# Late weights on GpSimd's queue, the split of the maxima on GpSimd, and PSUM banks divided 3 + 2 in a two-layer cross-attention kernel

## Chip, cores and metric

The kernel runs on one core of a Trainium2 chip. The metric is the time of one execution on the device in microseconds (us), the median of several runs. Lower is better.

## What is computed

Four batches of `x` (256 x 256) and a context (512 x 256) go through two layers, all in float32:

```python
# layer 0: 16 heads of 16
q, k, v = LN1(x) @ q_w + q_b, ctx @ k_w + k_b, ctx @ v_w + v_b
attn = softmax(q k^T / 4 + mask)                    # per head, 256 x 512
h = x + (attn v) @ cproj_w + cproj_b
h = h + gelu(LN2(h) @ fc_w + fc_b) @ proj_w + proj_b      # 256 -> 1024 -> 256
# layer 1: one head of 256
p = softmax((h w_q^T)(ctx w_k^T)^T / 16)
out = h + alpha * (p (ctx w_v^T)) w_o^T
```

## The kernel before, in words

Float32 products are made of three products of split operands (high times high, high times low, low times high; `product` and `products`, lines L515 to L538). Scores of layer 0 are made of bf16 terms that small DMAs stack into `q_stack` and `k_stack` (SP, `stack_group`, L449: six DMAs of queries L436, one of the mask row L441, six of keys L447, for each group of four heads; a batch has four groups).

A group has eight slots, a batch 32, numbered from `START` = 7 to 38. In a slot PE makes the scores of tiles of the *next* group for their row maxima (`max_tile`, L570, into `s1`, two banks of PSUM), DVE takes the maximum (`take_max`, L1363), PE makes transposed scores of this group (`exp_tile`, L587, into `s2`, two banks), ACT takes their exponential (L1033), and in slots 1 and 3 PE multiplies with the values of the group before (`pv`, L598, into `om`). After the eighth maximum of a group (slot 5) DVE splits it into three bf16 parts by four small operations, each waiting for the one before (`split_max`, L1368 to L1381). In slot 6, behind its exp tile, PE transposes these (`max_rows`, L580, L584), and ACT copies them into rows of `q_stack` (L1024); the next group's exp tiles need them.

Beside it the tables at the top put other work into slots, and each engine runs its part in that order: projections of the next batch (`PRE_AT`, `V_AT`; for batch 1 `EARLY_AT`), through one bank `pre_ps`; the output path of the batch before (`POST_AT`, for batch 2 `LATE_AT`: OT normalise, NT/CP projection, ZT, F0 to F3 and PJ0 to PJ3 the MLP, CT context, HT/G/S/PT/PC/DL layer 1), through two banks `post_ps`, whose order is `POST_BANK`; in batch 0 the preparation of weights (`PREP_AT` on PE and ACT, `PREP_LOW_AT` on DVE). The last batch has its own tail (`TAIL_AT`). GpSimd (POOL) squares for the GELU (L1749), makes low parts (L1754, L1714, L1718, L1764), adds biases (L1736, L1741) and takes the power -0.5 (L1695).

The order around the start: SP issues 4 + 3 loads, then stacks groups 0 and 1 of batch 0, then four DMAs of a selection matrix (L471), loads for batch 1, group 2, six late weight loads (L476, L479), group 3, five more late loads (L481 to L485), then batch 1. ACT's `pre(1, U_Q)` (L989) waits until all stacked DMAs of batch 0 have landed, since they read the tile that it overwrites.

## Time and profile before

| | us |
|---|---|
| median of 3 runs | 321.09 |
| lowest, highest | 319.31, 323.21 |
| the profiled execution | 322.16 |
| its span, first to last instruction | 320.1 |
| mean granted clock of TensorE | 0.941 of 2.4 GHz |

Times of rows are in us from the span's start unless marked ns. "Idle before" is an engine's idle time ahead of an operation, and the arrow names what ended it. A busy PE is not a PE at its peak, since matmuls overlap.

### The profile page before, as it was taken

How to read it: one execution, taken by the hardware profiler on the slowest of the kernel's cores; microseconds unless marked ns; L12 is line 12 of the kernel's file. 1: busy time of each engine (PE TensorE's matmuls, PEld its weight loads, DVE VectorE, ACT ScalarE, POOL GpSimd, SP SyncE). 2: the span in 40 equal slices, each digit the busy share in tenths (PEclk: the TensorE clock that was granted, in tenths of full speed). 3: DMA queues.
4: the chain of work that ended last, by engine and by line, in shares of the span. 5: the costliest groups of instructions: out<-in, count | busy, mean ns of one | idle time of the engine just before them, and what ended most of it. 6: DMA issues, size and time to landing. Idle time of an engine off the chain costs nothing.

```text
span 320.1 us, 5574 instructions
## 1 busy us (share of the span) xinstructions
PE 274.5 (86%) x2073; PEld 196.7 (61%) x2073; DVE 217.0 (68%) x431; ACT 188.8 (59%) x351; POOL 87.2 (27%) x85
## 2 busy tenths in 40 slices
PE   1966875999797997998997979998999999789895
PEld 1751343576345684865775758664966786568884
DVE  5767874464867959876469678867478665364944
ACT  1643652655947587777454786966365787335722
POOL 2302000410301166670001487420030246053100
PEclk9995659695979999999999999999999999999999
DMA  5533244821153001114203011121030000000000
GB/s 172 167 122 64 82 136 137 244 70 61 61 156 127 6 28 62 64 59 131 68 33 100 15 54 59 52 82 44 34 133 0 2 0 2 2 1 0 2 33 33
DMA packets 23358, 21.60 MB, mean 67 GB/s; under 512 B 4516, under 2 KB 20468, under 8 KB 23332
## 3 DMA queue, kind: packets, MB, share of 16 engines
q1 hardware_dynamic: 20544, 17.06, 17.3%
q10 hardware_dynamic: 2788, 4.20, 3.9%
q8 instruction: 16, 0.26, 0.4%
q14 instruction: 10, 0.08, 0.1%
HBM read 10.50 MB, written 1.05 MB: 36 GB/s over the span
## 4 chain that ended last, share of the span: by engine, by line
PE 43%; DVE 18%; ACT 16%; SPq 11%; issue 5%; POOL 3%; ACTq 2%; DMA 1%; DVEq 0%
PE post_ps L532 7%; PE om L604 6%; PE pre_ps L519 6%; DVE neg_max L1365 5%; PE s L577 4%; SPq L447 4%; PE post_ps L536 4%; SPq L436 4%; PE s L594 4%; ACT probs L1033 4%; ACT q_stack L1024 2%; PE s L532 2%; DVE ft L1448 1%; PE post_ps L873 1%; POOL y_l L1754 1%
## 5 line engine op out<-in xcount | busy, mean ns | idle before, releaser
L1365 DVE TENSOR_REDUCE neg_max<-s 128x1 f32<-128x512 f32 x128 | 83.3, 683 | 16.1 <-PE s L577 15.3
L1033 ACT ACTIVATE probs<-s 128x512 f32<-128x512 f32 x128 | 75.6, 599 | 28.7 <-PE s L594 28.0
L577 PE MATMUL s<-k_stack,q_stack 97*128 97x512 bf16 x128 | 51.6, 431 | 12.0 <-DVE neg_max L1365 6.3
L594 PE MATMUL s<-q_stack,k_stack 109*128 109x256 bf16 x256 | 52.7, 291 | 6.2 <-ACT probs L1033 5.0
L594 PEld LDWEIGHTS s<-q_stack,k_stack 109*128 109x128 bf16 x256 | 21.5, 104 | 22.3 <-ACT probs L1033 7.5
L577 PEld LDWEIGHTS s<-k_stack,q_stack 97*128 97x128 bf16 x128 | 12.7, 102 | 36.5 <-DVE neg_max L1365 20.2
L604 PE MATMUL om<-probs,vals 128*17 128x256 f32 x512 | 34.9, 393 | 0.0
L1695 POOL TENSOR_TENSOR ln<-ln,minus_half 128x2 f32<-128x2 f32 x8 | 5.6, 702 | 66.2 <-DVE ln L1313 66.0
L604 PEld LDWEIGHTS om<-probs,vals 128*17 128x17 f32 x512 | 12.1, 98 | 13.9 <-issue 7.9
L1391 DVE TENSOR_TENSOR y_l<-post_ps,y_h 128x512 fp32r<-128x512 f32 x12 | 8.3, 690 | 16.9 <-ACT y_h L1047 16.9
L1024 ACT ACTIVATE q_stack<-om 13x1024 bf16<-13x1024 bf16 x16 | 16.3, 1016 | 5.1 <-PE om L584 4.7
L1047 ACT ACTIVATE y_h<-post_ps 128x512 fp32r<-128x512 f32 x12 | 7.0, 595 | 17.5 <-PE post_ps L536 14.2
L1448 DVE SCALAR_TENSOR_TENSOR ft<-ft,fx 128x512 f32<-128x512 f32 x9 | 12.0, 1331 | 6.8 <-POOL ft L1749 6.8
L1714 POOL TENSOR_TENSOR kf<-kf,kp 128x512 f32<-128x512 f32 x7 | 8.1, 1161 | 28.7 <-ACT kp L1016 28.7
L1754 POOL TENSOR_TENSOR y_l<-fx,y_h 128x512 fp32r<-128x512 f32 x9 | 11.6, 1286 | 14.5 <-ACT y_h L1086 14.5
L1749 POOL TENSOR_TENSOR ft<-fx 128x512 f32<-128x512 f32 x9 | 9.4, 1040 | 15.6 <-ACT fx L1060 15.6
L532 PE MATMUL post_ps<-aT_h,wf_h 128*128 128x256 f32 x48 | 13.6, 316 | 0.0
L532 PE MATMUL post_ps<-wp_h,y_h 128*128 128x256 f32 x48 | 13.5, 314 | 0.0
L1736 POOL TENSOR_TENSOR h<-h,cb 128x512 f32<-128x512 f32 x3 | 3.8, 1281 | 34.0 <-DMA h<-in_x_dram 34.0
L532 PE MATMUL post_ps<-aT_h,wf_l 128*128 128x256 f32 x48 | 11.8, 280 | 0.0
L532 PE MATMUL post_ps<-wp_l,y_h 128*128 128x256 f32 x48 | 11.8, 279 | 0.0
L1344 DVE SCALAR_TENSOR_TENSOR kf<-pre_ps,bk,mask_f 128x512 f32<-128x512 f32 x7 | 5.2, 747 | 7.8 <-PE pre_ps L519 7.7
(329 smaller groups left out, 705.1 us busy)
## 6 DMA issues: line engine op xcount, KB each, us to landing
k_stack<-kp SPq DMA_DIRECT2D x96, 64.0 KB
q_stack<-qp SPq DMA_DIRECT2D x90, 32.0 KB
cx<-in_ctx_dram SPq DMA_DIRECT2D x4, 512.0 KB, 4.5
pcx<-in_ctx_dram ACTq DMA_DIRECT2D x3, 512.0 KB, 3.7
xz<-in_x_dram SPq DMA_DIRECT2D x5, 256.0 KB, 2.9
raw_late<-in_L_xattn_fc_w_dram SPq DMA_DIRECT2D x1, 1024.0 KB, 5.1
raw_late<-in_L_xattn_proj_w_dram SPq DMA_DIRECT2D x1, 1024.0 KB, 9.6
h<-in_x_dram ACTq DMA_DIRECT2D x3, 256.0 KB, 2.7
```

The lines of the kernel that those rows point to most:

```text
L436: sp.dma_start(q_stack[i * HD:(i + 1) * HD, group(g), :], qp[rows_of(g), part, g // 2, :]).then_inc(stacked[g], 16)
L447: sp.dma_start(k_stack[i * HD:(i + 1) * HD, group(g), :], kp[rows_of(g), part, c, :]).then_inc(stacked[g], 16)
L519: mm = pe.matmul(o, wi(w[a], k), vi(v[c], k), start=start and k == 0 and i == 0, stop=stop and k == n - 1 and i == 2)
L532: pe.matmul(o, wi(w[a], k), vi(v[c], k), start=start and i == k == a == c == 0, stop=False)
L577: pe.matmul(s1[:, s % 2, :], q_stack[0:ROW_MAX, hd, chunk(t)], k_stack[0:ROW_MAX, hd, :], start=True, stop=True).then_inc(s1_full, 1)
L594: mm = pe.matmul(s2[:, s % 2, i * LQ:(i + 1) * LQ], k_stack[:, hd, chunk(k)], q_stack[:, hd, :], start=True, stop=True)
L604: mm = pe.matmul(om[32 * j:32 * j + VW, 0:LQ], vals[:, k, j * NG + g, :], probs[:, g % 2, j, k, :], start=k == 0, stop=k == TK - 1)
L1024: act.activation(q_stack[ROW_MASK:ROWS, g * GH:(g + 1) * GH, :], om_rows[ROW_MASK:ROWS, :].unsqueeze(1).to_broadcast([ROWS - ROW_MASK, GH, ...
L1033: act.activation(probs[:, g % 2, s // 2, k:k + 2, :], s2[:, s % 2, :].rearrange("p (k n) -> p k n", k=2), ACT.Exp).then_inc(s2_free, 1)
L1365: dve.tensor_reduce(neg_max[:, g % 2, s % 2, s // 2:s // 2 + 1], s1[:, s % 2, :], AX.X, ALU.max, negate=True).then_inc(s1_free, 1)
L1448: dve.scalar_tensor_tensor(f, f, 1.0 / GELU_CUBIC, fx[i % 3], ALU.add, ALU.mult).then_inc(cube, 1)
L1754: pool.tensor_tensor(lo, fx[i % 3], hi.bitcast(F32), ALU.subtract).then_inc(y_split, 1)
```

## The change

1. SP's selection matrix goes out as one DMA with a broadcast instead of four.
2. The eleven late weight loads leave SP's queue. GpSimd issues six behind its first `split_max`, four in slot 8 and one in slot 14.
3. `split_max` moves from DVE to GpSimd, first thing in its slot, with the same four operations.
4. `s1` has three banks (batch 3 and the first eight tiles use two of them), and a max tile waits for the tile that had its bank. `pre_ps` and `post_ps` become two banks `work_ps` that alternate in the order of PE's program; while PJ holds one, all others use the other. Each use waits until the use before it on its bank has been emptied.
5. Slots move by one to three in all tables. ctx transposes come ahead of the vector transposes at the start.

```diff
-PRE_AT = {7: U_CT, 8: U_CT + 1, 9: U_ZT, 11: U_Q, 14: U_K, 22: U_K + 1}
-V_AT = {36: 0, 38: 1}
+PRE_AT = {7: 0, 8: 1, 9: 2, 10: 3, 14: 4, 19: 5}
+V_AT = {37: 0, 38: 1}
-POST_AT = {7: "OT", 8: "NT", 9: "CP", 11: "ZT", 13: "F0", 15: "F1", 16: "F2", 19: "F3", 20: "PJ0",
-           21: "PJ1", 22: "CT0", 23: "PJ2", 24: "CT1", 25: "PJ3", 26: "CX", 27: "HT", 28: "G", 30: "S0",
-           31: "S1", 33: "PT0", 34: "PT1", 36: "PC", 37: "DL"}
+POST_AT = {7: "OT", 8: "NT", 9: "CP", 12: "ZT", 14: "F0", 15: "F1", 17: "F2", 19: "F3", 20: "PJ0", 21: "PJ1",
+           22: "CT0", 23: "PJ2", 24: "CT1", 25: "PJ3", 26: "CX", 27: "HT", 29: "G", 30: "S0", 31: "S1",
+           34: "PT0", 35: "PT1", 36: "PC", 37: "DL"}
-EARLY_AT = {7: 0, 8: 1, 9: 2, 11: 3, 14: 4, 22: 5}
+EARLY_AT = {8: 0, 9: 1, 10: 2, 12: 3, 15: 4, 22: 5}
-PREP_AT = {16: "WT", 18: "WO", 19: "WC", 21: "CB", 22: "WF0", 24: "WF1", 28: "WP0", 30: "WP1", 38: "END"}
-PREP_LOW_AT = {17: "WT", 19: "WO", 21: "WC", 22: "CB", 24: "WF0", 26: "WF1", 31: "WP0", 36: "WP1"}
+PREP_AT = {16: "WT", 18: "WO", 20: "WC", 21: "CB", 22: "WF0", 24: "WF1", 25: "WP0", 28: "WP1", 40: "END"}
+PREP_LOW_AT = {17: "WT", 19: "WO", 21: "WC", 23: "CB", 24: "WF0", 27: "WF1", 32: "WP0", 35: "WP1"}
...
-        s1 = ps("s1", [P, 2, 512])
+        s1 = ps("s1", [P, 3, 512])
-        pre_ps = ps("pre_ps", [P, 512])
-        post_ps = ps("post_ps", [P, 2, 512])
+        work_ps = ps("work_ps", [P, 2, 512])
+        spare_ps = s1[:, 2, :]
...
+                    for use in new:
+                        bank = 1 - held if held is not None else 1 - bank
+                        uses.append(use + (bank,))
+                        if use[0] == "post" and use[2] == W_PJ:
+                            held = bank
+                    if step == "PJ3":
+                        held = None
...
+        def await_bank(eng, kind, b, n):
+            bank = work_bank(kind, b, n)
+            on = [u for u in WORK if u[3] == bank]
...
+        def s1_bank(b, s):
+            return s % 2 if b == B - 1 or NS * b + s < SLOTS else (NS * b + s) % 3
...
-                for g in range(NG):
-                    sp.dma_start(k_stack[ROW_MAX:ROWS, group(g), :], sel[:]).then_inc(sel_in, 16)
+                sp.dma_start(k_stack[ROW_MAX:ROWS, :, :].rearrange("p (g h) n -> p g (h n)", g=NG),
+                             sel[:].rearrange("p h n -> p (h n)").unsqueeze(1).to_broadcast([3 * GH, NG, GH * LK])).then_inc(sel_in, 16)
...
-                for i, w in ((2, l1_v), (3, l1_o)):
-                    sp.dma_start(raw_l1[i], w.rearrange("(c p) n -> p c n", p=P)).then_inc(wo_in, 16)
-                for g in range(NG):
-
-                    sp.dma_start(raw_c[rows_of(g), g // 2, :], cproj_w.rearrange("(j x d) n -> x j d n", j=GH, x=NG)[g]).then_inc(wc_in, 16)
                 stack_group(0, 3)
-                sp.dma_start(raw_f, fc_w.rearrange("(c p) n -> p c n", p=P)).then_inc(wf_in, 16)
...
-                await_(pe, s1_free, n - 1)
+                await_(pe, s1_free, s1_before(b, SLOTS * g + s))
...
-                    if s == SPLIT_AT:
-                        split_max(nb, ng)
...
+            def attend(b, g, s):
+                nb, ng = ahead(b, g)
+                if s == SPLIT_AT and nb < B:
+                    split_max(nb, ng)
...
                 key_low(0, 1)
+                pool.wait_ge(dve_const, 2)
+                split_max(0, 0)
+                for i, w in ((2, l1_v), (3, l1_o)):
+                    pool.dma_start(raw_l1[i], w.rearrange("(c p) n -> p c n", p=P)).then_inc(wo_in, 16)
+                for g in range(NG):
+
+                    pool.dma_start(raw_c[rows_of(g), g // 2, :], cproj_w.rearrange("(j x d) n -> x j d n", j=GH, x=NG)[g]).then_inc(wc_in, 16)
+                for s in range(START):
+                    attend(0, 0, s)
...
+            def load_late(at):
+                if at == LOAD_AT:
+                    pool.dma_start(raw_f, fc_w.rearrange("(c p) n -> p c n", p=P)).then_inc(wf_in, 16)
+                    pool.dma_start(cb[:], cproj_b.rearrange("(o n) -> o n", o=1).partition_broadcast(P)).then_inc(bc_in, 16)
+                    pool.dma_start(pb[:], proj_b.rearrange("(o n) -> o n", o=1).partition_broadcast(P)).then_inc(bc_in, 16)
+                    pool.dma_start(alpha_c[:], alpha.partition_broadcast(P)).then_inc(bc_in, 16)
+                elif at == LOAD_AT + 6:
+                    pool.dma_start(raw_p, proj_w.rearrange("(c p) n -> p c n", p=P)).then_inc(wp_in, 16)
```

## Rows read from the trace of the kernel before

**Rows 1.** The page: busy time by engine, and the granted clock.

```profile
PE 274.5 (86%) x2073; PEld 196.7 (61%) x2073; DVE 217.0 (68%) x431; ACT 188.8 (59%) x351; POOL 87.2 (27%) x85
...
PEclk9995659695979999999999999999999999999999
```

**Rows 2.** Windows by stage: PE, PEld, DVE, ACT, POOL busy, clock, DMA share, GB/s.

```profile
55.00:93.00 38.00, 33.53 (x214) 19.97 (x214) 21.72 (x39) 25.19 (x44) 7.63 (x7) 0.78 0.41 129
93.00:160.00 67.00, 60.99 (x507) 44.05 (x506) 50.13 (x96) 45.10 (x86) 24.14 (x20) 1.00 0.22 69
```

**Rows 3.** Timeline of SP's queue: start, duration, instruction, count.

```profile
26.87 3.15 SPq L471 DMA_DIRECT2D k_stack<-fx  x4
...
40.54 0.59 SPq L476 DMA_DIRECT2D raw_late<-in_L_xattn_w_v_dram  x1
41.17 0.47 SPq L476 DMA_DIRECT2D raw_late<-in_L_xattn_w_o_dram  x1
41.68 2.42 SPq L479 DMA_DIRECT2D raw_late<-in_L_xattn_cproj_w_dram  x4
...
48.70 3.74 SPq L447 DMA_DIRECT2D k_stack<-kp  x6
```

**Rows 4.** The chain that ended last, at its first piece on L471.

```profile
26.87 0.83 SPq L471
```

**Rows 5.** Timelines of PE and ACT, 38 to 60 us.

```profile
38.52 0.39 PE L594 MATMUL s<-q_stack,k_stack 109*128 109x256 bf16 x2 [0.25 <-ACT probs L1033]
39.66 0.32 PE L584 MATMUL om<-ident_b,max_cols 128*109 128x128 bf16 x2 [0.76 <-DVE max_cols L1381]
...
42.31 1.04 PE L577 MATMUL s<-k_stack,q_stack 97*128 97x512 bf16 x2 [1.67 <-DMA k_stack<-kp]
...
56.51 0.61 PE L594 MATMUL s<-q_stack,k_stack 109*128 109x256 bf16 x2 [3.81 <-ACT probs L1033]
...
54.40 0.84 ACT L994 ACTIVATE qf<-pre_ps,bq 128x256 f32<-128x256 f32 x2 [4.69 <-DMA k_stack<-kp]
```

**Rows 6.** Windows of 2 us after the two stalls.

```profile
42.00:44.00 2.00, 1.69 (x7) 1.11 (x8) 1.95 (x4) 0.14 (x1) 0.00 (x0) 0.50 0.81 261
...
58.00:60.00 2.00, 2.00 (x7) 1.22 (x7) 0.29 (x1) 0.27 (x1) 1.16 (x1) 0.50 0.58 131
```

**Rows 7.** Groups of the page by line: the first and last operation of DVE's split.

```profile
L1375 DVE CAST max_cols<-neg_max 128x8 bf16<-128x8 f32 x16 | 3.6, 226 | 0.6
...
L1381 DVE TENSOR_TENSOR max_cols<-max_rest,max_cols 128x8 bf16<-128x8 f32 x16 | 2.8, 178 | 0.6
```

**Rows 8.** Tile `max_cols`: who waited for the split, us and times.

```profile
  PEld om L584: 8.5, 9
  PE om L584: 5.7, 9
```

**Rows 9.** POOL's timeline: small operations, the power, and two widths of tensor_tensor.

```profile
1.25 0.29 POOL L1770 TENSOR_SCALAR_AFFINE_SELECT ident<-ident 128x128 f32<-128x128 f32 x1 [0.24 <-POOL sel_small L1768]
1.50 0.18 POOL L1773 TENSOR_SCALAR_AFFINE_SELECT sel_small<-sel_small 12x4 f32<-12x4 f32 x1
...
40.83 0.72 POOL L1695 TENSOR_TENSOR ln<-ln,minus_half 128x2 f32<-128x2 f32 x1 [13.15 <-DVE ln L1313]
...
131.65 1.76 POOL L1741 TENSOR_TENSOR h<-h,pb 128x512 f32<-128x512 f32 x1
136.46 1.27 POOL L1754 TENSOR_TENSOR y_l<-fx,y_h 128x512 fp32r<-128x512 f32 x1 [3.05 <-ACT y_h L1086]
...
141.45 2.38 POOL L1764 TENSOR_TENSOR pc_l<-pcx,pc_h 128x1024 fp32r<-128x1024 f32 x1 [0.68 <-ACT pc_h L1098]
```

**Rows 10.** What PE waited for from 93 to 160 us.

```profile
PE s L577 <- DVE neg_max L1365: 2.7, 6, 1.1
PE pre_ps L553 <- DVE cT_l L1335: 0.7, 1, 0.7
...
PE om L584 <- DVE max_cols L1381: 0.6, 2, 0.3
```

More of the change, by code:

```diff
@@ L315, in pre_use, with work_uses @@
             return PRE_USES * b + pre_place(b, n) + 1
+        def work_uses():
+            uses, bank, held = [], 1, None
+            for n in FIRST_ORDER:
+                if pre_place(0, n) % 3:
+                    uses.append(("pre", 0, n, pre_place(0, n) % 3 - 1))
+            for b in range(B):
+                for at in range(START, LAST_SLOT if b == B - 1 else START + NS):
+                    new = []
+                    if b < B - 1 and at in pre_at(b + 1):
+                        new.append(("pre", b + 1, pre_at(b + 1)[at]))
+                    if b < B - 1 and at in V_AT:
+                        new.append(("pre", b + 1, U_V + V_AT[at]))
+                    step = steps_at(b - 1).get(at) if b > 0 else None
+                    new += [("post", b - 1, n) for n in STEP_USES.get(step, ())]
+                    if b == 0 and PREP_AT.get(at) in PREP_USES:
+                        new.append(("prep", 0, PREP_AT[at]))
+                    for use in new:
[5 more added lines that the diff above has]
+                        held = None
+            return uses
@@ new lines, in s1_bank, with s1_before, s2_bank, s2_before @@
+        def s1_bank(b, s):
+            return s % 2 if b == B - 1 or NS * b + s < SLOTS else (NS * b + s) % 3
+        def s1_before(b, s):
+            n = NS * b + s
+            return max([i for i in range(max(0, n - 3), n) if s1_bank(i // NS, i % NS) == s1_bank(b, s)], default=-1) + 1
+        def s2_bank(b, s):
+            return s % 2
+        def s2_before(b, s):
+            n = NS * b + s
+            return max([i for i in range(max(0, n - 3), n) if s2_bank(i // NS, i % NS) == s2_bank(b, s)], default=-1) + 1
@@ L1695, in rstd, with split_max @@
                 pool.tensor_tensor(st[:, :, 8], st[:, :, 8], minus_half[:], ALU.pow).then_inc(done, 1)
+            def split_max(b, g):
+                step = 3 * (NG * b + g)
+                part = [max_cols[:, :, ROW_MAX + i:ROWS:3] for i in range(3)]
+                neg = neg_max[:, g % 2, :, :]
+                pool.wait_ge(s1_free, NS * b + SLOTS * (g + 1))
+                await_(pool, rows_ps, NG * b + g)
+                pool.tensor_copy(part[0], neg).then_inc(max_step, 1)
+                pool.wait_ge(max_step, step + 1)
+                pool.tensor_tensor(max_rest[:], neg, part[0], ALU.subtract).then_inc(max_step, 1)
+                pool.wait_ge(max_step, step + 2)
+                pool.tensor_copy(part[1], max_rest[:]).then_inc(max_step, 1)
+                pool.wait_ge(max_step, step + 3)
+                pool.tensor_tensor(part[2], max_rest[:], part[1], ALU.subtract).then_inc(max_split, 1)
+            def attend(b, g, s):
+                nb, ng = ahead(b, g)
+                if s == SPLIT_AT and nb < B:
+                    split_max(nb, ng)
             def mask_row_of(b):
@@ L1810, in tail_slot @@
                     tail(step)
-            def iteration(b, first, last):
-                for at in range(START, START + NS):
+            def load_late(at):
[6 more added lines that the diff above has]
+                    pool.dma_start(raw_p, proj_w.rearrange("(c p) n -> p c n", p=P)).then_inc(wp_in, 16)
+            def iteration(b, first, last):
+                for at, ab, g, s, attends in slots(b, last):
+                    if attends:
+                        attend(ab, g, s)
+                    if first:
+                        load_late(at)
                     if not last and at == LN1_AT:
```

140 lines of the change are left out of this document (72 added, 68 removed).

## The prediction

> **What bounds the kernel now.** Read the page first: PE is busy 86% of the span, the others at most 68%, and the granted clock falls to about half in several slices of the first 93 us, then stays at full [rows 1]. Then the windows by stage. A full batch (93 to 160 us) takes 67.0 us with PE busy 61.0, so there PE sets the pace and some 6 us of it are waits. Batch 0's stage from 55 to 93 has PE busy 33.5 of 38 at a mean clock of 0.78 [rows 2]. So the middle has little air, and the start has much. SP's queue then shows the start: it issues DMAs back to back, here from 26.87 to 52.4 us, and between the stacks of groups 1, 2 and 3 lie the selection matrix (four, 3.15 us) and six late weights (0.59 + 0.47 + 2.42, with gaps 3.60 us) [rows 3]. Two waits come of that: PE stands 1.67 us at 42.31 for keys of group 2, and ACT stands 4.69 us until 54.40 for group 3's keys before it may overwrite the query tile; PE stands 3.81 us behind ACT's exponentials [rows 5]. After each, PE runs at 0.50, the lower of its two levels (1.2 GHz) [rows 6].
>
> **The change part by part** (terms against the profiled execution, 322.16 us, 1.07 above the median; span 320.1, the rest lies around it).
>
> *SP's queue.* Six issues go: 3.60 us. Three of four selection issues go: 3.15 less one of 0.83 [rows 4], 2.3 us, if one DMA of four times the rows issues like one of them; if it issued like all four, nothing. So group 2's last keys come 2.3 us earlier than 42.3 and group 3's land 5.9 us before 54.3, at 48.4. The queries of batch 1 move from slot 11 to 12, which at the pace of the rows is about 49 us, so ACT then waits for nothing or under 1 us. PE gets back 1.67 + 3.81 = 5.5 us. Bounds: 3 (selection saves nothing, and what comes next is the PE product in front of ACT's wait) and 5.5. What is late next is the pace of PE, DVE and ACT inside the slots. The five later loads moved off SP stand behind group 3, ahead of batch 1's stacks, which wait for their parts anyway: 0.
>
> *Clock.* The exp tile at 56.51 and six key matmuls behind it run at half speed until about 61.4: 4.9 us of PE work, 2.4 if PE never went idle. After the first stall PE also runs low, from 42 to 48, but short gaps (0.76 and 0.25 us at 38.5 to 39.7 [rows 5]) stay, so I take 0.6 of up to 2.8. Together -3.0, bounds 0 and -5.2.
>
> *The split on GpSimd.* No row shows these operations there. Before, four of about 0.2 us [rows 7] and their hand-overs, 0.85 us from the last maximum to PE's transpose. GpSimd's tensor_tensor takes 1.27 us at 512 and 2.38 at 1024 elements [rows 9]: 2.2 ns an element and 0.16 fixed, so 0.18 at 8 elements, as its 12x4 operation takes 0.18. Its hand-over is up to 0.24. A split is then 4 x 0.18 + 3 x 0.24 + 0.1 = 1.5 us, 0.65 more. Bounds: 0 more (hand-overs as short as DVE's), and like the power's 0.72 each [rows 9], 3.7 us, 2.85 more; below nothing by 0.3 a group where DVE was late itself (0.6 us for two groups [rows 10]). I take 0.65, nearest the rows of like size. PE waited for the split in 9 of 16 groups [rows 8]; the other seven had cover (a projection or output product in slot 6). Two of the nine lie before 42 us: +1.3, now on the path. One is in the rest of batch 0, two in each of the two full batches, two in the last: each +0.65. Queued behind the waiting split on GpSimd are squares, low parts and biases; in slot 21 the order is bias (1.76 us), key rest, split, low part of F2, and DVE and PE's PJ2 wait for that last one. DVE gives up 0.85 x 16 = 13.6 us of a 217 us engine, which alone moves nothing.
>
> *GpSimd's DMAs.* The first six follow the first split, about 32.3, and the second split is due at 39.66 less 0.85 = 38.8 [rows 5]: 6.5 us for six issues. On SP these took 0.47 to 0.6 [rows 3], 3.6 in all, and hide. Above 1.1 us each they delay the second split. No row shows an issue on GpSimd; bounds 0.4 and 2.4 us (its longest operation [rows 9]), the first costing 0, the second 14.3 - 6.5 = 7.8 us. I take under 1.1, cost 0. The four of slot 8 have until the query rest, two slots later at least. The Trainium skill ("DMA: Bandwidth & Descriptors", sections Specifications and SWDGE vs HWDGE vs iDMA) says that a DMA from GpSimd has its descriptors written by software there, about 1 us to the first byte against 0.6; and ("SBUF — State Buffer", Who interferes with whom) that certain copies on VectorE lock it out meanwhile. If those 0.4 us more stood on GpSimd for each issue, six would take 6.0 and the sum stays; the second rule speaks against the change, and no row of before can show it, since GpSimd issues nothing there.
>
> *Banks.* PE waits 2.7 us of a full batch for a maximum to free one of two score banks [rows 10]; with three, I take all of it as gone. Against it, shared work banks: in slot 7 the second OT transpose now waits for the context part to be drained, where PE waited 0.7 us for DVE's cT_l one step later [rows 10]; F1 waits for the keys' drain, PJ0 for the second keys'. I take +0.7 for the first, 0 for the others, which have a whole product as cover. Per full batch: -2.7 + 0.7 + 2 x 0.65 = -0.7, two of them -1.4; bounds -3.3 and +3 each (two missed drains of 1.5 us). The last batch keeps two score banks: 2 x 0.65 less 0.6 for a freer DVE, +0.7, bounds -1 and +2.
>
> *Rest of batch 0.* DVE's splits go and the weight steps are spread, and PE's score banks are three, with one split +0.65: I take -1.0 net, bounds 0 and -3. The remaining slot moves by one are taken at 0.
>
> Sum: -5.5 + 1.3 - 3.0 - 1.4 + 0.7 - 1.0 = **-8.9 us**. 322.2 - 8.9 = 313.3 for an execution like the profiled one, 1.1 less against the median: **312.2 us**. About 1% (3.2 us) is what a measurement of this kernel can tell from no change.
>
> **The rivals.**
> (a) *Only the stalls go.* The lower clock stays where it was, because PE still has short gaps, and splits and banks cancel: -5.5 + 1.3 and nothing else, 317. For it: the clock fell to about half four separate times in the first 93 us, some without a long stall [rows 1]. Against: PE was really idle for 3.8 us before the second [rows 5].
> (b) *GpSimd's queue is late with DMAs.* At 2 us an issue the second split is 5.5 us late, and PE with it, which eats the stall: 312.2 + 5.5 = 317.7, and the four of slot 8 could cost as much again, 321. For it: no row of its issues. Against: SP's rows.
> (c) *Shared work banks bite.* +3 us instead of -0.7 in both full batches: 312.2 + 7.4 = 319.6. For it: DVE drains late where it is full.
> (d) *Slower: GpSimd's split costs like its power.* 2.85 more instead of 0.65 for each of the nine exposed groups is +19.8, and I let the seven covered ones pay half of 2.85, +10.0: 312.2 + 29.8 = 342. It decides from 0.65 + 8.9 / 9 = 1.6 us more than DVE, 0.63 us an operation. For it: the two-element power at 0.72. Against: 0.18 for a 12x4 operation, and two widths of tensor_tensor that extrapolate to it [rows 9]. The Trainium skill ("GPSIMD Engine Reference", Performance versus the Vector engine) puts an elementwise operation at about twice VectorE's time; a split of 1.7 us would add 0.2 to each of nine groups and give 314.0. No row of before shows GpSimd at 8 elements in a tensor_tensor.
>
> **How the numbers follow.** The forecast, with its own range of 305 to 316.5, 0.58; (a) 0.14; (b) 0.10; (c) 0.08; (d) 0.10, since it decides at a price between two rows. Faster by over 1% (under 317.9): 0.58 + 0.12 of (a) + 0.05 of (b) + 0.01 of (c) = 0.76. Within 1%: 0.02 + 0.04 + 0.06 + 0.01 of (d) = 0.13. Slower: the rest, 0.11. The range is 303 (stalls, clock and banks all at their good ends would be under 300, together unlikely) to 320, which leaves (d) and a little of (b) and (c) outside.
>
> **What would show it.** SP's queue free by about 47 to 49 us; no wait of ACT over 1 us at the query step of batch 1, none of PE for keys of group 2; exp of slot 13 near 52; clock not at 0.5 from 56 to 61. GpSimd's four split operations about 0.2 us each, and the time from the last maximum to PE's transpose about 1.5 us. In a full batch, DVE's maxima no longer end a wait of PE, and the batch takes 66 to 66.5 us. It is wrong if GpSimd's issues fill the time to its second split, if full batches take over 68 us, or if ACT waits at another place for what SP now sends earlier.

## The result, and the profile after

The changed kernel takes **317.93 us** (median of 20 runs, 314.11 to 321.68) against 319.76 us of the kernel before (20 runs beside it, 318.43 to 323.21); the ratio is 0.9885, 95% interval 0.9851 to 0.9919, so some 3.7 us (1.2%) less. A ratio leaves out the runs of the slower of this kernel's two states (8 of these 20), so it can differ from the ratio of two medians, and where they differ it is the ratio that a reading rests on. The forecast was 312.2 us, 8.9 us less. The time lies in its range, but the gain is less than half of what was put down.

The profiled execution after takes 315.73 us with a span of 313.5, against 322.16 and 320.1. So the pair of traces shows 6.6 us, more than the medians (1.8) or the ratio (3.7) do: the one after is among the shortest of its runs, the one before is 2.4 us over its median of 20. Sizes are therefore read below from several profiles, never from this pair alone.

The page of the kernel after, its parts 1 and 2:

```profile
PE 272.2 (87%) x2073; PEld 198.5 (63%) x2073; DVE 207.1 (66%) x367; ACT 188.3 (60%) x351; POOL 110.3 (35%) x160
...
PEclk9999579987889999999999999999999999999999
```

DVE lost 9.9 us and POOL gained 23.1 (15.5 the split's 64 operations, 7.6 the eleven DMA issues): that work moved as planned [rows 1]. PE is still the pace. Six slices lie below full clock, as before, but they are less deep: up to the transpose of slot 38 the mean clock is 0.87 (0 to 95.5 us) against 0.81 (0 to 98.4 us). The windows of the two full batches, to be set beside [rows 2]:

```profile
95.50:160.60 65.10, 59.40 (x498) 44.73 (x497) 45.67 (x78) 43.97 (x85) 27.66 (x35) 1.00 0.20 63
160.60:226.90 66.30, 59.96 (x499) 44.75 (x498) 46.16 (x79) 44.06 (x85) 28.32 (x36) 1.00 0.17 57
```

SP's queue after, with one issue for the selection rows (0.88 us, against 3.15 for four in [rows 3]) and group 3's keys at 44.66, where they had begun at 48.70:

```profile
27.86 0.88 SPq L538 DMA_DIRECT2D k_stack<-fx  x1
...
44.66 3.75 SPq L515 DMA_DIRECT2D k_stack<-kp  x6
```

ACT and PE there, to be set beside [rows 5]: ACT's wait at the query step is 2.24 us for 4.69, PE's wait for keys of group 2 is 0.48 for 1.67, and its wait for ACT 1.91 for 3.81.

```profile
52.53 0.84 ACT L1058 ACTIVATE qf<-work_ps,bq 128x256 f32<-128x256 f32 x2 [2.24 <-DMA k_stack<-kp]
```

```profile
42.75 0.60 PE L640 MATMUL s<-k_stack,q_stack 97*128 97x512 bf16 x2 [0.48 <-DMA k_stack<-kp]
...
54.65 0.39 PE L657 MATMUL s<-q_stack,k_stack 109*128 109x256 bf16 x2 [1.91 <-ACT probs L1097]
```

GpSimd's timeline: the second split, and ahead of it the six DMA issues that stand behind the first split.

```profile
33.26 0.95 POOL L1861 DMA_DIRECT2D raw_late<-in_L_xattn_w_v_dram  x1
34.21 0.73 POOL L1861 DMA_DIRECT2D raw_late<-in_L_xattn_w_o_dram  x1
34.94 2.52 POOL L1864 DMA_DIRECT2D raw_late<-in_L_xattn_cproj_w_dram  x4
40.62 0.20 POOL L1750 CAST max_cols<-neg_max 128x8 bf16<-128x8 f32 x1 [3.17 <-DVE neg_max L1429]
40.91 0.20 POOL L1752 TENSOR_TENSOR max_rest<-neg_max,max_cols 128x8 f32<-128x8 f32 x1
41.18 0.20 POOL L1754 CAST max_cols<-max_rest 128x8 bf16<-128x8 f32 x1
41.46 0.21 POOL L1756 TENSOR_TENSOR max_cols<-max_rest,max_cols 128x8 bf16<-128x8 f32 x1
```

An operation is 0.20 us and the next starts 0.28 later: 1.1 us for an undisturbed split, where 1.5 was forecast. The six issues end at 37.5, 3.2 us before the split is due.

What PE waited for over the whole span (engine, line, releaser, total us, times, longest):

```profile
PE om L647 <- POOL max_cols L1756: 10.2, 7, 2.1
...
PE s L640 <- DVE neg_max L1429: 4.2, 14, 0.6
PE work_ps L702 <- DVE cT_l L1399: 3.5, 2, 1.8
```

The first line is the surprise: fewer waits for the split than before (7 for 9) and nearly twice the time (10.2 for 5.7 us, [rows 8]). If a split is only 0.25 us longer than on DVE (1.1 for 0.85), something else is late. The third line has no counterpart before. The timelines of POOL, DVE and PE at 82 us, and of PE at 99, show both:

```profile
82.34 1.13 POOL L1750 CAST max_cols<-neg_max 128x8 bf16<-128x8 f32 x1 [3.35 <-DVE neg_max L1429]
```

```profile
82.19 1.21 DVE L1543 SCALAR_TENSOR_TENSOR wp_l<-raw_late,wp_h 128x1024 fp32r<-128x1024 f32 x1
```

```profile
84.37 0.32 PE L647 MATMUL om<-ident_b,max_cols 128*109 128x128 bf16 x2 [2.12 <-POOL max_cols L1756]
...
99.03 0.66 PE L702 MATMUL work_ps<-ident,oT 128*128 128x128 f32 x4 [1.77 <-DVE cT_l L1399]
```

GpSimd's cast of 8 elements lasts 1.13 us and ends (83.47) just after DVE's subtraction (83.40), which had started 0.15 earlier. The kernel before has the same thing the other way round: DVE's cast of 8 elements takes 0.57 us twice (132.88 and 199.8) where the other fourteen take 0.18, and the first ends (133.45) just after the bias on GpSimd, which runs from 131.65 to 133.41 [rows 9].

```profile
132.88 0.57 DVE L1375 CAST max_cols<-neg_max 128x8 bf16<-128x8 f32 x1
```

That is why the mean of this cast stands at 226 ns in [rows 7], beside 178 for the last operation of the split. And in the changed kernel's slot 7 the second transpose of the output path takes the bank that a projection product has just filled, and waits 1.77 us until DVE has drained it.

### The profile page after: what moved, and what is told of

Read it like the earlier page. It is cut to its first block, busy times and chain, and to the rows that moved or that the text cites. A ratio compares the mean times of both kernels' runs of the same rounds, so it can differ in the third digit from the quotient of the medians.

```text
span 313.5 us, 5588 instructions
## 1 busy us (share of the span) xinstructions
PE 272.2 (87%) x2073; PEld 198.5 (63%) x2073; DVE 207.1 (66%) x367; ACT 188.3 (60%) x351; POOL 110.3 (35%) x160
## 3 DMA queue, kind: packets, MB, share of 16 engines
q0 software_dynamic: 1152, 3.15, 3.3%
HBM read 10.50 MB, written 1.05 MB: 37 GB/s over the span
## 4 chain that ended last, share of the span: by engine, by line
PE 52%; POOL 10%; ACT 10%; SPq 10%; DVE 7%; issue 6%; DMA 2%; ACTq 2%; POOLq 0%; DVEq 0%
PE work_ps L590 10%; PE om L667 7%; PE work_ps L577 6%; PE s L640 5%; PE work_ps L594 5%; PE s L657 5%; SPq L515 5%; SPq L504 3%; DVE neg_max L1429 3%; ACT probs L1097 2%; POOL y_l L1820 2%; PE s L590 2%; POOL kf L1780 1%; ACT q_stack L1088 1%; DMA k_stack<-kp 1%
## 5 line engine op out<-in xcount | busy, mean ns | idle before, releaser
L640 PE MATMUL s<-k_stack,q_stack 97*128 97x512 bf16 x128 | 49.3, 418 | 6.6 <-DVE neg_max L1429 4.2
L657 PEld LDWEIGHTS s<-q_stack,k_stack 109*128 109x128 bf16 x256 | 20.9, 103 | 21.1 <-ACT probs L1097 6.6
L1750 POOL CAST max_cols<-neg_max 128x8 bf16<-128x8 f32 x16 | 5.5, 344 | 66.4 <-DVE neg_max L1429 66.4
L1111 ACT ACTIVATE y_h<-work_ps 128x512 fp32r<-128x512 f32 x12 | 7.2, 597 | 16.2 <-PE work_ps L594 14.5
L1440 DVE TENSOR_TENSOR y_l<-work_ps,y_h 128x512 fp32r<-128x512 f32 x12 | 8.3, 688 | 12.0 <-ACT y_h L1111 12.0
L1497 DVE SCALAR_TENSOR_TENSOR ft<-ft,fx 128x512 f32<-128x512 f32 x9 | 10.0, 1110 | 6.5 <-POOL ft L1815 6.5
L647 PE MATMUL om<-ident_b,max_cols 128*109 128x128 bf16 x32 | 5.0, 241 | 10.2 <-POOL max_cols L1756 10.2
L590 PE MATMUL work_ps<-wp_h,y_h 128*128 128x256 f32 x48 | 13.3, 310 | 0.5 <-DVE kf L1408 0.5
L590 PE MATMUL work_ps<-aT_h,wf_h 128*128 128x256 f32 x48 | 12.8, 300 | 0.0
L1408 DVE SCALAR_TENSOR_TENSOR kf<-work_ps,bk,mask_f 128x512 f32<-128x512 f32 x7 | 5.2, 746 | 10.6 <-PE work_ps L577 10.3
L590 PE MATMUL work_ps<-wp_l,y_h 128*128 128x256 f32 x48 | 11.8, 279 | 0.0
```

What stands on the lines that cost most here:

```text
L590: pe.matmul(o, wi(w[a], k), vi(v[c], k), start=start and i == k == a == c == 0, stop=False)
L640: pe.matmul(s1[:, s1_bank(b, SLOTS * g + s), :], q_stack[0:ROW_MAX, hd, chunk(t)], k_stack[0:ROW_MAX, hd, :], start=True, stop=True).then_ ...
L657: mm = pe.matmul(s2[:, s2_bank(b, SLOTS * g + s), i * LQ:(i + 1) * LQ], k_stack[:, hd, chunk(k)], q_stack[:, hd, :], start=True, stop=True)
```

## The experiments

All times below are medians. Each group of kernels was measured beside runs of the kernel before, which the third column gives; only kernels with the same one can be compared directly. What tells most are the places of the maxima's transposes in each profile, for they cut the span into stages: the one of slot 22 and of slot 38 of batch 0, the same slot of the next batches, the last one, and the end. (The one of slot 14 is left out, since the new slots move a projection step across it.)

| kernel | us | before | slot 22 | to slot 38 | full batches | last rows | to the end |
|---|---|---|---|---|---|---|---|
| before | | | 77.2 | 21.2 | 66.9, 66.9 | 28.2 | 59.7 |
| after | 317.93 | 319.76 | 72.7 | 22.8 | 65.1, 66.3 | 29.1 | 57.5 |
| e_ctrl | 318.03 | 321.5 | 71.1 | 23.4 | 66.5, 66.3 | 29.1 | 57.5 |
| e_vec_first | 318.37 | 321.5 | 71.6 | 24.6 | 66.0, 67.6 | 29.1 | 57.5 |
| e_fc_sp | 318.59 | 321.5 | 71.6 | 24.8 | 66.2, 67.7 | 29.1 | 57.4 |
| e_split_dve | 319.44 | 321.5 | 71.5 | 20.6 | 67.7, 68.8 | 28.2 | 58.3 |
| e_banks_back | 318.81 | 321.16 | 73.3 | 24.6 | 65.9, 65.9 | 29.1 | 57.5 |
| f_sp_only | 314.19 | 321.16 | 70.0 | 19.6 | 67.0, 66.9 | 28.2 | 59.7 |
| e_pre_late | 315.71 | 321.16 | 71.8 | 23.4 | 64.3, 66.6 | 29.1 | 57.5 |
| e_wp33 | 315.79 | 321.16 | 72.2 | 22.9 | 66.6, 66.3 | 29.1 | 57.5 |
| h_pool | 319.30 | 320.99 | 69.9 | 22.0 | 68.0, 68.0 | 29.1 | 59.4 |
| h_hyb | 319.50 | 320.99 | 70.0 | 23.1 | 68.0, 68.1 | 29.1 | 59.4 |
| h_new | 315.17 | 320.99 | 73.5 | 20.9 | 64.4, 66.6 | 29.1 | 57.5 |
| f_sp_again | 315.90 | 320.99 | 70.0 | 21.0 | 67.0, 66.9 | 28.2 | 59.8 |
| g_best | 310.75 | 320.14 | 72.2 | 21.8 | 64.4, 66.4 | 29.1 | 57.6 |
| g_dve_old | 320.70 | 320.14 | 71.9 | 23.1 | 68.2, 68.0 | 28.2 | 57.8 |
| g_tail | 313.56 | 320.14 | 72.0 | 22.2 | 66.9, 67.0 | 28.1 | 57.7 |
| g_late33 | 314.00 | 320.14 | 71.6 | 23.7 | 64.4, 66.5 | 29.1 | 57.5 |

The two columns of batch 0 scatter by 1 to 2 us each between profiles of one kernel (f_sp_only and f_sp_again, after and e_ctrl), with the clock. Together they scatter more: g_tail has the batch 0 of f_sp_only, and its slot 38 stands at 94.2 where those two have 89.6 and 91.0. The last two columns agree within 0.1.

**The changed kernel once more (e_ctrl).**

> The changed kernel once more, unchanged. Its profiled execution had a clock of 0.962 and a span 6.6 us under the one profiled before, while the medians differ by 1.8 us and the ratio is 0.9885. Theory (the runs scatter with the granted clock): a ratio of 0.985 to 0.992, and a second profile whose span is 2 to 5 us longer, at a clock of 0.93 to 0.95, with the difference before 100 us. Rival (the profiled pair is typical): ratio 0.98 and the same span within 1 us.

318.03 us, ratio 0.9892 (0.9843 to 0.9941). The same time again, so the missing 5 us is no chance of the first runs. Its ratio and clock (0.950) are the theory's, but its span is not: 313.9 us, 0.4 longer than the first profile's, as the rival had it. New in its profile is a stretch at half clock right behind the wait of slot 7, which the first profile didn't have. Its 2 us windows, PE's busy time first and the clock in the third column from the end:

```profile
96.00:98.00 2.00, 0.23 (x3) 0.05 (x1) 0.79 (x2) 1.15 (x2) 0.00 (x0) 1.00 0.00 0
98.00:100.00 2.00, 2.00 (x8) 1.38 (x9) 1.31 (x5) 0.57 (x1) 0.00 (x0) 0.53 0.03 8
100.00:102.00 2.00, 2.00 (x12) 1.88 (x11) 1.38 (x3) 0.78 (x3) 0.00 (x0) 0.62 0.59 223
```

PE stands almost still from 96 to 98, then works at 0.53. That makes the full batch 1.4 us longer than in the first profile (66.5 for 65.1).

**Three guesses: the start's order, four loads, the split.**

```diff
 # e_vec_first: the vector rows' transpose goes ahead of pre(0, U_CT), as before the change
 # e_fc_sp: SP issues these again, behind group 3's stack
-                if at == LOAD_AT:
-                    pool.dma_start(raw_f, ...)   # and cb, pb, alpha_c
+                sp.dma_start(raw_f, ...)         # and cb, pb, alpha_c
 # e_split_dve: the whole of split_max runs on VectorE again
-                if s == SPLIT_AT and nb < B:
-                    split_max(nb, ng)            # GpSimd
+                    if s == SPLIT_AT:
+                        split_max(nb, ng)        # VectorE, after its maxima
```

> The changed kernel, with the vector transposes ahead of the context transposes again. Theory: the early start of PE at 4.9 us is what leaves the key product at 11.1 us at the lower clock (0.43 us from matmul to matmul where it was 0.23), so the keys' first DMA goes out 0.9 us later; undone, the first six-fold key stack starts at 14.6 instead of 15.6 and the kernel gains about 1 us. Rival: the clock there is chance, and nothing moves.

> The changed kernel, with fc_w, cb, pb and alpha back on SP's queue behind group 3's stack (the six first late loads and proj_w stay on GpSimd). Theory: the 1 MB of fc_w issued at 42.5 us travels ahead of group 3's stack and makes its last DMA land 4.5 us after its issue instead of 2.4; back behind it, ACT's wait at the query step of batch 1 falls from 2.2 us to under 0.5 and the kernel gains 1.5 to 2 us. Rival: the landing is slow because of the small stacking DMAs themselves; nothing moves.

> The changed kernel, with the split of the maxima back on DVE (same slots, banks and queues; GpSimd waits for the first split before its six loads). Theory: on GpSimd a split costs PE 0.3 to 1.1 us more at each of the 7 groups where it waits, and 2.1 us once where a two-input DVE operation blocks it, so the kernel gains 3 to 4 us. Rival: DVE needs its 0.85 us a group itself, and the kernel loses 2 us or more.

318.37, 318.59 and 319.44 us: ratios 0.9874, 0.988 and 0.9864, each interval over the others. The first two theories fall: slot 22 comes at 71.6 with both, 71.1 without. The first key stack of six starts at 15.01 us in e_vec_first and in e_ctrl alike, and ACT's wait at the query step is 1.82 us in e_fc_sp for 1.80 in e_ctrl, both ended by PE. The third is the telling miss. With the split on DVE the end of batch 0 comes 2.4 to 3.4 us earlier (92.1 for 94.5 and 95.5), as expected, but the full batches take 67.7 and 68.8 us (65.1 to 66.5 in the two profiles of the changed kernel). The gain is given back there, and the 3 to 4 us that were expected don't come.

**What each part does alone (e_banks_back, f_sp_only, e_pre_late, e_wp33).**

```diff
 # e_banks_back
-        s1 = ps("s1", [P, 3, 512])
-        work_ps = ps("work_ps", [P, 2, 512])
+        s1 = ps("s1", [P, 2, 512])
+        work_ps = ps("work_ps", [P, 3, 512])     # bank 2 for projections, POST_BANK for the rest
 # f_sp_only, from the kernel before
-                for g in range(NG):
-                    sp.dma_start(k_stack[ROW_MAX:ROWS, group(g), :], sel[:]).then_inc(sel_in, 16)
-                sp.dma_start(raw_l1[i], ...)     # and the four of raw_c
+                sp.dma_start(k_stack[ROW_MAX:ROWS, :, :]..., sel[:]...to_broadcast(...)).then_inc(sel_in, 16)
+                pool.wait_ge(max_split, 1)       # GpSimd, at the end of its prologue
+                pool.dma_start(raw_l1[i], ...)   # and the four of raw_c
 # e_pre_late
-PRE_AT = {7: 0, 8: 1, 9: 2, 10: 3, 14: 4, 19: 5}
+PRE_AT = {8: 0, 9: 1, 10: 2, 11: 3, 14: 4, 19: 5}
 # e_wp33, in PREP_LOW_AT
-32: "WP0"
+33: "WP0"
```

> The changed kernel with the banks of the kernel before: two banks for the maxima's scores, one bank of their own for the projections, two for the output path. The slots' new order, the late weights on GpSimd's queue and the split on GpSimd stay. Theory (the shared banks cost about what the third bank brings): the wait of 1.77 us of the transpose of slot 7 for VectorE's cT_l goes back to some 0.7, no stretch at half clock follows at 98 to 106, the waits for neg_max of 2.7 us a batch come back, a full batch takes 66 to 67 us (65.1 and 66.3 in the changed kernel) and the time is 317 to 320 us. Rival one (the third bank is a gain of 1.4 us and more): 319.5 to 321. Rival two (the shared banks are the loss that ate the forecast): 314 to 316.5, and less scatter between runs.

> The kernel before with the changes on SyncE's queue alone: one DMA for the selection rows, and the six late weight loads issued by GpSimd after the first split; the split on VectorE, the banks and the slots as before. Theory (this part carries nearly all of the gain, and the rest of the change sums to about nothing): the wait of 4.69 us of ScalarE at the query step falls to about 2, the transpose of group 2's maxima comes at 54 to 55 us where before it came at 59.9, the full batches keep 66.9 us, and the time is 315.5 to 317.5 us, 3.5 to 5.5 under the kernel before. Rival (the banks and GpSimd's split bring the gain of the full batches, and this part alone 1 to 2 us because the clock gives the rest back): 318.5 to 320.

> The changed kernel with the four first projection steps of the batches ahead one slot later (slots 8 to 11 in place of 7 to 10), so that the second transpose of the output path in slot 7 no longer takes the bank that a projection product has just filled. Theory (the shared bank's wait of 1.77 us at 99 and 164 us is a real loss and sets off the half clock that follows in some executions): the wait falls under 0.7 us, no slice at half clock at 98 to 106, a full batch takes 64 to 65 us, and the time is 314.5 to 316.5 us with less scatter. Rival (the wait only moves to the next bank user in slot 8 or 9, or the late projections are missed by the group after them): 317.5 to 320.

> The changed kernel with VectorE's subtraction for the low part of the projection weights one slot later (slot 33 in place of 32), so that it doesn't run beside GpSimd's first cast of the split at 82 us. Theory (the two engines block each other there): that cast takes 0.2 us in place of 1.13, TensorE's wait for the split at 84.4 falls from 2.12 to about 1.2 us, and the rows of the maxima that stand at 84.4 move by about 0.9; in the time about 0.9 us, which is near what the rounds can tell. Rival (the cast is late for another reason, its wait for the last max or the queue of GpSimd): it still ends at the same time and the wait stays 2.1.

*f_sp_only*: 314.19 us, 7.0 under the kernel before by the medians and 3.5 by the ratio (0.9891, 0.9829 to 0.9952); measured again it has 315.90, 5.1 under by the medians and 5.2 by the ratio (0.9838, 0.9787 to 0.989). Its slot 38 is 8.8 and 7.4 us earlier than before (4.2 in g_tail), and nothing else moves: full batches of 67.0 and 66.9. ACT's wait at the query step is down to 1.05 us, and what ends it is no longer a DMA:

```profile
51.13 0.84 ACT L989 ACTIVATE qf<-pre_ps,bq 128x256 f32<-128x256 f32 x2 [1.05 <-PE pre_ps L514]
```

PE's wait for ACT there, 3.81 us before and 1.91 and 1.47 in the two profiles of the changed kernel, is 0.16. So SP's part alone gives about as much as the whole change or more. Which of the two, these runs leave open: its medians are 2 to 4 us lower and its spans (311.4, 312.9) 0.6 to 2.5 us shorter than those of the changed kernel (313.5, 313.9), but the two never ran side by side, and the intervals of their ratios overlap (0.9891 and 0.9838 against 0.9885 and 0.9892). It leaves out of the change the split, the banks, the slots and the five later loads' move.

*e_banks_back*: 318.81 us, ratio 0.9988 (0.9933 to 1.0043). The theory's numbers hold: slot 7's wait is 0.7 us, PE's waits for `neg_max` come back (2.0 us in a full batch, where the changed kernel has 1.0 and the kernel before 2.7), and the full batches take 65.9 and 65.9 against 65.1 to 66.5. In the full batches third score bank and shared work banks cancel, nearly. Its ratio is 1% above the changed kernel's all the same, and in its profile that lies in batch 0 (slot 38 at 97.9); whether the banks help there stays open.

*e_pre_late*: 315.71 us (0.9925, 0.988 to 0.997), so in the range by its time, while the ratio shows no gain over the changed kernel's 0.9885. The waits of its first full batch:

```profile
PE s L640 <- DVE neg_max L1429: 1.5, 2, 1.2
PE om L647 <- POOL max_cols L1756: 1.4, 1, 1.4
PE work_ps L577 <- DVE zT_l L1399: 1.1, 1, 1.1
```

L702 is gone from the list; 1.1 us of it is back at the query product, which now starts one slot nearer its operand. The batch takes 64.3 us, the shortest of all until then. The second takes 66.6, no less than the changed kernel's 66.3, for there the waits that come back (1.1 for `zT_l`, 0.6 more for `neg_max`, 0.7 for `z`) eat the gain. And the clock: six profiles have the wait of slot 7, each of them twice. Behind seven of these twelve waits PE runs at half clock within 1.5 us, behind four of the first and three of the second. Of the twelve profiles without this wait (the kernel before among them) none shows half clock at this place. Only g_dve_old shows any in the full batches, both times right at the end of a wait of 2.5 us for the split in slot 22, and e_split_dve has the same once. That such a wait brings the clock down in some executions is as near shown as profiles can.

*e_wp33*: 315.79 us (0.9934, 0.9888 to 0.998), again no gain by the ratio. POOL's cast and PE's transpose:

```profile
82.23 0.20 POOL L1750 CAST max_cols<-neg_max 128x8 bf16<-128x8 f32 x1 [3.70 <-DVE neg_max L1429]
```

```profile
83.34 0.32 PE L647 MATMUL om<-ident_b,max_cols 128*109 128x128 bf16 x2 [1.55 <-POOL max_cols L1756]
```

With DVE's subtraction out of the way the cast takes 0.20 us again and PE waits 1.55 for 2.12, 0.6 less. Two later profiles with the same edit, g_late33 and h_new, have 1.19 and 1.20, the 0.9 less that was expected; with the split on DVE it is 0.92. So the two engines do hold each other up there, and of the 1.2 us that PE waits longer than before 0.9 come from it.

**Which engine suits which slots (h_pool, h_hyb, h_new, f_sp_again).** h_pool is f_sp_only with `split_max` on GpSimd; h_hyb and h_new have it on either:

```diff
+                    if s == SPLIT_AT and nb < 1:              # VectorE
+                if s == SPLIT_AT and nb < B and nb > 0:       # GpSimd
```

h_hyb is otherwise f_sp_only, h_new otherwise the changed kernel with the edits of e_pre_late and e_wp33.

> The kernel before with the changes on SyncE's queue and, on top, the split on GpSimd in every batch; banks and slots as before. Theory (the split on GpSimd is what costs in batch 0: it reaches TensorE later there, and the gaps bring stretches at half clock, while it takes work from VectorE in the full batches): against the kernel with the queue's changes alone (transposes of the maxima at 79.5 and 89.6 us, full batches of 67.0 and 66.9 us) the transpose at 89.6 comes 2 to 6 us later, the full batches take 66 us each, and the time is 316 to 319 us. Rival (the loss of batch 0 comes from the shared banks and the new slots): 312.5 to 314.5, under the kernel with the queue's changes alone.

> As the kernel before with the queue's changes, with the split on VectorE in batch 0 and on GpSimd from batch 1 on; banks and slots as before. Theory (the split costs in batch 0 and gains 1.0 us in each full batch and perhaps as much in the last): batch 0 as with the queue's changes alone (89.6), full batches of 66 us, time 311.5 to 313.5 us, the lowest so far. Rival (the full batches' gain was that of the slots' new order, not of the split): 313.5 to 316.

> The changed kernel with the three parts that cost it taken back: the split on VectorE in batch 0 and on GpSimd from batch 1 on, the first projection steps one slot later, and the low part of the projection weights one slot later. Theory (each of them was seen alone: batch 0 ends at 92.1 with the split on VectorE, a full batch takes 64.3 us with the late projections): rows of the maxima at 92, full batches of 64.3 and 66.6 us, time 311 to 313.5 us. Rival (the parts don't sum, because the clock of batch 0 falls somewhere else): 314 to 316.

> The same kernel as the one with the queue's changes alone, measured again with the others of this call. Theory (this part alone makes 7 us of the 321, since its first measurement had 314.19 against 321.16): median of 313.5 to 316 and 5 to 8 us under the kernel before of the same call. Rival (the six runs of the first measurement were lucky in their clock): 316 to 318.5.

*h_pool*: 319.30 us (0.9971, 0.9935 to 1.0007), 3.4 over f_sp_again beside it (0.9838, 0.9787 to 0.989), which is clear of the noise. Slot 22 comes at 69.9, as without the split on GpSimd, and slot 38 2.3 and 0.9 us later than in the two profiles of SP's part alone (2 to 6 were expected); but a full batch takes 68.0 us, one more than with the split on DVE, where one less was expected. *h_hyb*: 319.50 (0.9985, 0.9947 to 1.0022), outside both ranges and 6 us over the theory's, partly of my own making: the splits of batch 1's first two groups are made in batch 0's slots, and `nb < 1` leaves just these on GpSimd. PE stands 2.12 us behind the blocked cast at 80.7 there too. Its full batches, again 68.0 and 68.1, are the rival's: on the old slots GpSimd's split is a loss throughout. *h_new*: 315.17 us (0.9739, 0.9668 to 0.981). Its median lies in the rival's range, 1.7 us over the theory's, and its ratio rests on three runs; its full batches are as expected, but slot 38 stands at 94.4 where 92 was expected, and slot 22 at 73.5, though all splits up to there are on DVE.

**The missing cell, the tail, and a version that beats both (g_dve_old, g_tail, g_late33, g_best).**

```diff
 # g_dve_old: e_banks_back and e_split_dve together
 # g_tail: f_sp_only with the changed kernel's TAIL_AT and LATE_AT
 # g_late33: e_pre_late and e_wp33 together
 # g_best: e_pre_late, e_vec_first, batch 0's slots (EARLY_AT, PREP_AT, PREP_LOW_AT) as before, and
+                    if s == SPLIT_AT and NG * nb + ng < NG + 2:                 # VectorE
+                if s == SPLIT_AT and nb < B and NG * nb + ng >= NG + 2:         # GpSimd
```

> The changed kernel with the banks of the kernel before and the split on VectorE: what is left of the change is SyncE's part and the new slots. Theory (the new slots suit the split on GpSimd, with the steps before the transpose moved to where VectorE was free, and it is the pair that brings the full batches from 68.0 to 65.9 us): full batches of 67 us, time 316 to 318.5 us. Rival (the new slots gain by themselves): full batches of 66 us or less, time 314 to 316.

> The kernel before with SyncE's changes and the new slots of the last batch and of what follows it, all else as before. Theory (the 2.2 us that the changed kernel gains behind the last row of the maxima, 57.5 us against 59.7, are those slots' own): 57.5 us there and a time of 312.5 to 314.5 us, some 2 under the kernel with SyncE's changes alone. Rival (they need the third bank or the split off VectorE): 59 to 60 us there, and 314 to 316.

> The changed kernel with two table entries moved: the first projection steps one slot later, and the low part of the projection weights in slot 33 in place of 32; the split stays on GpSimd in every batch. Theory (the two blocks each cost what their traces show, 1.77 us twice less what comes back, and 0.9, and each sets off half clock in some runs): rows of the maxima at 93 to 95 us at the end of batch 0, full batches of 64.3 and 66.6, time 313.5 to 315.5 us. Rival (the parts don't sum): 315.5 to 318, as each of the two alone.

> The changed kernel with batch 0 as it was (vector rows first, the slots of the kernel before, the split on VectorE for the six groups whose maxima are taken there), and with its own slots, third score bank and GpSimd split from then on, the first projection steps one slot later. Theory (the parts gain and cost where the trace put them, so they sum): the transpose that came at 89.6 and 91.0 us with the queue's changes alone comes at 89.5 to 92, the full batches take 64.3 and 66.6, the rows of the last batch 29.1 and what follows 57.5 us, so a span of 307 to 310 and a time of 309.5 to 312 us, the lowest of all. Rival (the queue's changes and the rest don't sum, since the clock of batch 0 decides): 313 to 316.

*g_dve_old*: 320.70 us (1.0016, 0.9984 to 1.0048), no faster than the kernel before and over the ranges of theory and rival, and so are its full batches with 68.2 and 68.0 us. The cells of a full batch (us, mean of two, one profile each where nothing else is said) are then:

| | split on VectorE | split on GpSimd |
|---|---|---|
| old slots, old banks | 67.0 (four profiles) | 68.0 (two profiles) |
| new slots, old banks | 68.1 | 65.9 |
| new slots, new banks | 68.3 | 65.7 to 67.0 (five profiles) |

In a full batch neither the slots nor the split gain alone; each loses 1 us, and together they gain 1.1 with the old banks. (The cells of new slots with the split on VectorE hold stretches at half clock, one a batch, which are part of the loss; so do four of the five profiles in the last cell.) Why, DVE's timeline of g_dve_old shows, with POOL's beside it:

```profile
128.46 0.76 DVE L1437 CAST max_cols<-neg_max 128x8 bf16<-128x8 f32 x1
129.26 1.18 DVE L1439 TENSOR_TENSOR max_rest<-neg_max,max_cols 128x8 f32<-128x8 f32 x1
130.47 1.09 DVE L1441 CAST max_cols<-max_rest 128x8 bf16<-128x8 f32 x1
131.59 0.18 DVE L1443 TENSOR_TENSOR max_cols<-max_rest,max_cols 128x8 bf16<-128x8 f32 x1
```

```profile
128.02 1.17 POOL L1776 TENSOR_TENSOR kf<-kf,kp 128x512 f32<-128x512 f32 x1 [0.75 <-ACT kp L1078]
129.15 1.26 POOL L1816 TENSOR_TENSOR y_l<-z,y_h 128x512 fp32r<-128x512 f32 x1
130.37 1.15 POOL L1780 TENSOR_TENSOR kp<-kf,kp 128x512 bf16<-128x512 f32 x1
```

The new slots bring GpSimd's wide operations right beside the split. On DVE each of three small operations ends only when one of them has ended (129.22, 130.44 and 131.56 against 129.19, 130.41 and 131.52), and PE waits 2.5 us. On GpSimd the split stands in that same queue and can't meet them, but it meets DVE's: its first cast takes 0.67 us at this place in the changed kernel (129.98 to 130.65, beside an operation of DVE that ends at 130.59), and PE waits 1.39. On the old slots it stands there behind the bias of 1.74 us (h_pool, 125.21), and PE waits 1.15 where it waited 0.34.

*g_tail*: 313.56 us (0.9781, 0.9734 to 0.9828), 57.7 us behind the last row for 59.7: the tail's gain is its new slots' own. PE at 272 to 284 us before had waits of 0.64, 0.71, 0.47, 0.69 and 0.71 us; 3.2 together; g_tail and the profile after have four at these places (0.38, 0.47, 0.33 and 0.31 in g_tail), 1.5. *g_late33*: 314.00 us (0.9817, 0.9765 to 0.9869), within its expectation (its slot 38, 95.3, is not) and under the changed kernel by two table entries: 3.9 us by the medians, 2.2 by the ratios, whose intervals just overlap. *g_best*: **310.75 us** (309.75 to 313.34; ratio 0.9719, 0.9674 to 0.9765), 9.4 under the kernel before, the only kernel here whose whole interval lies over 2% under the kernel before, and under the change by 7 us by the medians and 5 by the ratios. Its stages came as expected but for batch 0, 94.0 for 89.5 to 92, in a profiled execution that was the slowest of its six.

## Why the prediction was wrong

- **SP's queue, -5.5: right in kind, too large.** SP was free at 48.4, as put down. But up to slot 38 PE is idle 22.2 us before and 18.2 to 18.6 in the three profiles with SP's part alone (f_sp_only, f_sp_again, g_tail): 3.6 to 4.0 us for 5.5. In the changed kernel the two stalls are 0.48 + 1.91 us where they were 1.67 + 3.81, so 3.1 of the 5.5 came back. ACT's wait at the query step was to be under 1 us; it is 2.24, ended by a DMA that landed 4.1 us after the last key issue (in the kernel before 2.0), and 1.80 in e_ctrl, ended by PE.
- **The clock, -3.0: right in kind.** Half clock at 56 to 61 us is gone in both profiles of the changed kernel. PE's busy time up to slot 38, 76.2 us before, is 71.3, 72.8 and 75.6 with SP's part alone, 0.6 to 4.9 less. The whole was sized on one execution, 2.4 us over the median of 20 runs, that had much half clock to lose.
- **First splits, +1.3: about half of it.** 1.1 us each for 1.5; PE waits 1.98 and 1.03 us in e_ctrl for 1.62 and 0.76, +0.6 together, and in h_pool nothing of it is left at slot 22.
- **GpSimd's DMAs at no cost: right, and rival (b) falls.** 0.54 to 0.95 us an issue, all hidden.
- **Rest of batch 0, -1.0: this step failed.** It should have gained and it cost. By the sum (-5.5 + 1.3 - 3.0 - 1.0) slot 38 was to come 8.2 us earlier, at 90.2; it comes 2.9 and 3.9 earlier, at 95.5 and 94.5, and that is more than the whole of the miss, since what lies behind it came 3.7 and 2.3 us shorter than before, where -0.7 was put down. Against SP's part alone (89.6, 91.0, 94.2), where +0.3 was put down, these two and e_pre_late (95.2), whose batch 0 has the same slots, are 4 us later at the median, and PE is idle for 19.8, 21.1 and 22.4 us instead of 18.2 to 18.6. Two causes are seen in the traces.
  - The split: I priced it by its own duration and the queue ahead of it, and not by what the other engine does at that moment: blocked, it took 2.0 us from its first start to its end for 1.05 (82.34 to 84.31, 40.62 to 41.67), and PE's wait is 2.12 for 0.92. The Trainium skill says it: "SBUF — State Buffer", section Who interferes with whom, has an instruction of VectorE with two inputs in SBUF contend with one of GpSimd that reads there, and whoever issues second wait for the whole of the other. The 1.13 us for 0.20 beside `wp_l` agree, and so do the 1.18 us the other way round. The prediction named another rule of that section, for DMAs, and held that no row of before could show it; for the split, the cast of 0.57 us beside the bias could.
  - The new slots and banks, which I took at 0 or as a gain here: PE waits 1.2 to 1.3 us for ACT's exponentials near 79 us, also where the splits up to there are on DVE (1.18 in e_split_dve and h_new; 0.80 in g_dve_old; 0.25 in f_sp_only). And slot 22 comes at 71.1 to 73.5 in all eleven kernels with the new slots of batch 0, on whichever engine the split is, at 72.2 in g_best, which has only the new banks there, and at 69.9 to 70.0 in four of the five with the old slots, the old banks and SP's changes, h_pool and h_hyb among them (g_tail 72.0).
  - How the loss divides is not shown: from slot 22 to 38 seven profiles with the split on DVE have a median of 21.2 us (19.6 to 23.1), the eight with GpSimd's blocked cast 23.4 (22.0 to 24.8), the three with GpSimd and the subtraction moved 22.9 (20.9 to 23.7). So moving the block away gives back 0.5 of the 2.2 us there; the rest would be the longer split, gaps of the slots, and PE at half clock behind both.
- **Full batches, -0.7 each: right in sum, by luck.** Measured -1.8 and -0.6 in the first profile, -0.4 and -0.6 in the second. The third score bank was put at -2.7 and gives 1.0: between e_banks_back and the changed kernel the waits for `neg_max` go from 2.0 to 1.0 us in the first full batch (2.0 to 1.6 in the second). The shared work banks were put at +0.7; the waits for `cT_l` go from 0.7 + 0.3 to 1.8 + 0.5 us, so +1.3, and in most profiles half clock too. The splits, put at +1.3, are one wait of 1.4 for 0.6, +0.8, of which 0.5 is a cast of 0.67 us. These come to +1.1; what paid for them was the slots, which I took at 0 and which are worth 2.1 us a batch once the split is on GpSimd. Rival (c) had the right place, but its sum falls.
- **Last batch, +0.7:** +0.9 to the last row, then -2.2 from the tail's new slots, also taken at 0.
- **Rivals (a) and (b)** gave the time best (317 and 317.7), but for wrong reasons: the clock's gain came and GpSimd's issues were hidden, and other parts ate the gain. Rival (d) falls by the 0.20 us.

In sum SP's part, put at -8.5 us, gave 5 to 7 us by the medians and 3.5 to 5.2 by the ratios. What remained of the change, forecast at -0.4 us, cost 2 to 4 us by the medians and up to 1.7 by the ratios; by the traces it costs about 4 us ahead of slot 38 and gives 2.4 to 3.9 back behind it. Shown by an edit of its own are the block at slot 30 (0.9 us of PE's wait, e_wp33, h_new and g_late33), slot 7's wait (e_pre_late, 0.8 and 2.2 us of the first full batch against the two profiles of the changed kernel, nothing of the second), and the tail's slots (g_tail, 2 us). Open is how much of batch 0 belongs to the slots, the banks and the split, and how much of its clock to which gap: profiles of one kernel differ there by more than the parts do.

## What to carry to other kernels

Price a small operation that moves to another engine by what both engines run at that moment: beside a wide operation of the other engine 0.2 us became 1.1 to 1.2, whichever side it was on. The trace of before may show it already, in the longest of a group. Slots, banks and engines tuned together can't be judged one at a time; a two by two table of runs showed that two edits that each lose 1 us of a full batch gain 1 together. And when a large change gives little, run its surest part alone: here that was as fast as the whole or faster.

## What the runs showed of the hardware

- A small operation's duration in the profile holds its wait for the other engine: `max_cols<-neg_max` is 0.20 us at least on GpSimd and 1.13 at most, and 0.18 and 0.57 on VectorE in the kernel before. The wait isn't shown as idle time. Look at the longest of a group, not only its mean.
- GpSimd at 128x8 is nearly as fast as VectorE: 0.20 to 0.21 us against 0.17 to 0.18 where neither is held up, and 1.1 against 0.85 us for the split; two wide shapes had extrapolated to 0.18.
- SP's issue of the selection rows with four times the rows took 0.88 us for 0.83 [rows 4]: here its price was that of an issue, not of its rows.
- Behind the same wait of 1.77 us the clock falls in some executions and not in others (in e_ctrl at 98 us and not in the first profile; behind 7 of 12 such waits in all): a wait's cost has a part that one trace may not show.
